# Attention scores through one query-key layer, both images in row tiles, in a software-pipelined token kernel

## The reference

```python
# 1 tokens of an image (192 channels, 14x14 patches)
loc  = dwconv(gelu(conv(x, pl_w, stride=16)))          # layer "L"
g    = gelu(conv(wavelet_packet(x), pg_w1)); g = gelu(dwconv(g))   # layer "G"
glob = conv(g, pg_w2)                                  # layer "W2"
h = (1 - gate) * loc + gate * glob
h = relu(dwconv(h)); h = relu(dwconv(h)); h = dwconv(loc + h)      # "F1", "F2", "F3"
h = concat(cls, layernorm(h) * ln_g + ln_b, txt)       # T = 325 tokens
# 2 attention in a band of 64 tokens, no softmax
n = layernorm(h)
q, k, v = (gelu(n @ w1 + b1) @ w2 + b2 for each of q, k, v)
scores = (q @ k.T) / sqrt(192 * 64) * mask             # mask: 0 <= i - j < 64
h = h + layernorm(scores @ v)
# 3 feed-forward with quantized tokens and ternary weights, hidden width 512
z = rmsnorm(layernorm(h)) ; up, gate = split(quant(z) @ ternary(w_in))
h = h + quant(rmsnorm(silu(gate) * up)) @ ternary(w_out)
```

## Time and profile before

| | |
|---|---|
| median of 3 runs | 1199.82 us (1197.52 to 1203.08) |
| span of the profiled execution | 1195.4 us |
| TensorE busy | 1081.3 us (90% of the span) |
| VectorE busy | 1033.5 us (86%) |
| ScalarE busy | 963.3 us (81%) |
| GpSimd busy | 812.7 us (68%) |

### The profile page before, as it was taken

The page is one execution under the profiler, slowest core; times in us unless marked ns, Lnnn a source line. Parts: engine busy times, 40 slices in busy tenths (PEclk is TensorE's granted clock), DMA queues, the critical chain, the costliest instruction groups (busy, mean ns, idle before and its releaser), DMA issues.

```text
span 1195.4 us, 19559 instructions
## 1 busy us (share of the span) xinstructions
PE 1081.3 (90%) x5674; PEld 736.5 (62%) x5674; DVE 1033.5 (86%) x3013; ACT 963.3 (81%) x2437; POOL 812.7 (68%) x860
## 2 busy tenths in 40 slices
PE   6877999999999999999999999999999897878544
PEld 3655676767676767677676757676766655545311
DVE  1887598999999999999999999999999997856653
ACT  4656687899989898989999988989898978766543
POOL 4446486868687777878686868787786857562521
PEclk9898999999999999999999999999999998979655
DMA  8101010101010100101010101001010000000000
GB/s 327 62 27 41 8 41 7 50 7 57 9 57 9 46 17 16 49 13 50 13 53 7 56 9 54 9 16 50 16 47 15 10 11 15 10 15 9 9 12 14
DMA packets 21513, 40.25 MB, mean 34 GB/s; under 512 B 2656, under 2 KB 18208, under 8 KB 19104
## 3 DMA queue, kind: packets, MB, share of 16 engines
q1 hardware_dynamic: 21408, 39.01, 9.4%
HBM read 31.02 MB, written 7.99 MB: 33 GB/s over the span
## 4 chain that ended last, share of the span: by engine, by line
PE 76%; DVE 9%; ACT 7%; issue 4%; POOL 2%; DMA 1%; SPq 0%; POOLq 0%; DVEq 0%; ACTq 0%
PE bank L398 14%; PE bank L517 7%; PE bank L428 7%; PE bank L439 4%; PE bank L430 4%; PE bank L438 4%; PE bank L376 4%; PE bank L377 3%; PE bank L539 3%; PE bank L458 3%; PE bank L459 3%; DVE bank L1214 2%; PE bank L471 2%; PE bank L472 2%; PE bank L587 2%
## 5 line engine op out<-in xcount | busy, mean ns | idle before, releaser
L1214 DVE SCALAR_TENSOR_TENSOR bank<-padA,c_col,bank 128x406 f32<-128x406 f32 x560 | 357.9, 639 | 7.6
L398 PE MATMUL bank<-x_sb,w_emb 128*128 128x392 f32 x576 | 216.6, 507 | 6.5 <-ACT padA L755 3.7
L810 ACT ACTIVATE prod<-padB,c_col 128x196 f32<-128x196 f32 x432 | 174.3, 449 | 5.1 <-POOL accB L1734 2.5
L1703 POOL TENSOR_TENSOR yg<-y_f,c_gout 128x512 f32<-128x512 f32 (+1 forms) x96 | 122.6, 1278 | 45.9 <-DVE y_f L1404 45.8
L398 PEld LDWEIGHTS bank<-x_sb,w_emb 128*128 128x128 f32 x576 | 102.3, 192 | 60.8 <-ACT padA L755 5.6
L810 ACT ACTIVATE early<-padB,c_col 128x196 f32<-128x196 f32 x288 | 120.7, 449 | 2.3 <-POOL accB L1734 2.2
L517 PE MATMUL bank<-w_in,xq 128*128 128x512 bf16 (+1 forms) x384 | 109.1, 411 | 13.6 <-ACT xq L873 13.6
L1696 POOL TENSOR_TENSOR s<-s,c_mhalf 128x1 f32<-128x1 f32 (+1 forms) x96 | 55.2, 575 | 90.8 <-ACT s L886 90.8
L867 ACT ACTIVATE yq<-bank 128x512 bf16<-128x512 f16 (+1 forms) x96 | 50.2, 523 | 50.8 <-PE bank L529 50.8
L879 ACT ACTIVATE th<-bank,sm 128x512 f32<-128x512 f32 (+1 forms) x96 | 65.3, 681 | 31.6 <-PE bank L517 31.1
L1385 DVE SCALAR_TENSOR_TENSOR ya<-th,bank 128x512 f32<-128x512 f32 (+1 forms) x96 | 65.1, 678 | 26.5 <-ACT th L879 26.3
(11 more groups left out here) (219 smaller groups left out, 3229.3 us busy)
## 6 DMA issues: line engine op xcount, KB each, us to landing
x_sb<-xt SPq DMA_DIRECT2D x16, 1176.0 KB, 5.3
out<-o_sb SPq DMA_DIRECT2D x64, 96.0 KB
w_sq<-squares SPq DMA_DIRECT2D x1, 3840.0 KB, 15.6
h_sb<-txt SPq DMA_DIRECT2D x32, 51.8 KB
out<-o_sb SPq DMA_DIRECT2D x32, 51.8 KB
h_sb<-txt SPq DMA_DIRECT2D x32, 44.2 KB
w_in<-win SPq DMA_DIRECT2D x1, 1024.0 KB, 17.6
c_row<-broads SPq DMA_DIRECT2D x1, 672.0 KB, 19.2
```

What stands on the lines that cost most here:

```text
L398: done = mm(pE[:, 0:2 * N_PATCH], w_emb[:, k, m, :], x_sb[:, k, :], start=k == 0, stop=k == KC - 1)
L810: made = go(grid(prod[ACC[s] ^ 1][:, k, :]), tap_view(padB[min(s, 2)], SIDE, k), ACT.Copy, scale=tapcol(s, 1, k))
L1214: v.scalar_tensor_tensor(grid(acc if k == TAPS - 1 else run), tap_view(pad, ROWS_A, k), tapcol(s, 0, k), grid(run), ALU.mult, ALU.add).the ...
L1703: g.tensor_tensor(yg[0:m, :], y_f[0:m, :], c_gout[0:m, :], ALU.mult).then_inc(f_yg, 1)
```

## The change

- The second query layer q2 goes, with `queries_out`, the tile `q2` and its zeros. Since `q @ k.T = (hq Wq + bq) (hk Wk + bk)^T`, with `hq` and `hk` the hidden layers, a key row becomes `hk (Wk Wq^T)` plus a bias, and is multiplied with `hq` itself; what depends on the key alone is an offset for each key, `hk (Wk bq) + bk.bq`.
- The product of the two weight matrices is made once on the chip: `query_key_weights` on TensorE (transposes of both matrices, the product, the bias columns), after `layer_W2` of pair 0, and `query_key_blocks` on VectorE (copies out of PSUM), after `token_scale_3` and `ternary_weights` and ahead of `mix` of pair 0. The result takes the place of `kw2` in `w_sq`.
- `scores(a)` now makes both images: first nine small products for the key offsets (one or two columns), then, tile by tile, a product over 128 channels for each image and one over 64 partitions (a row tile) for each image, image 0 into one bank and image 1 into the other. The offsets lie in the bank that `values_out(1)` frees.
- VectorE gets `key_offsets` (two small operations, which wait for the scores of image 0), and `scores_out` adds the offset and multiplies by the mask in one operation with a pointer operand.
- The attention now has 23 units, 18 of them ScalarE's (before 26 and 21).
- The lists of all five engines are laid anew. `DEPTH` is 8; the pipeline's stages have the same distances, turn 0 now only loads.

The core of the diff:

```diff
-U_XT, U_Q1, U_K1, U_V1, U_Q2, U_K2, U_V2, U_SC, U_Y = 0, 3, 6, 9, 12, 15, 18, 21, 23
-UNITS = 26
-ACT_UNITS = 21
+U_XT, U_Q1, U_K1, U_V1, U_K2, U_V2, U_SC, U_Y = 0, 3, 6, 9, 12, 15, 18, 20
+UNITS = 23
+ACT_UNITS = 18
...
-            def scores(a, img):
-
-                if img == 0:
-                    took(a, U_K2 + 2)
-                unit_free(a, U_SC + img)
+            def scores(a):
+
+                took(a, U_K2 + 2)
+                unit_free(a, U_SC)
+                for t in range(TILES):
+                    r = pT[U_SC % 2][0:ROWS[t], R_AT + 2 * t:R_AT + 2 * t + 2]
+                    mm(r, hk[:, 2, tok_cols(t)], c_qk[:, 0:2], start=True, stop=False)
+                    for img in range(2):
+                        mm(r[:, img:img + 1], hk[:, img, tok_cols(t)], c_qk[:, 2:3], start=False, stop=img == 1)
+                unit_free(a, U_SC + 1)
                 at = 0
                 for t, n in ((0, SEAM), (1, P + ROWS[2]), (2, ROWS[2])):
-                    dst = pT[(U_SC + img) % 2][0:ROWS[t], at:at + n]
+                    dst = [pT[(U_SC + img) % 2][0:ROWS[t], at:at + n] for img in range(2)]
                     q = slice(t * P, t * P + n)
-                    mm(dst, k2[:, img, tok_cols(t)], q2[:, img, q], start=True, stop=False)
-                    done = mm(dst, k2[:, 2, tok_cols(t)], q2[:, 2 + img, q], start=False, stop=True)
+                    for img in range(2):
+                        mm(dst[img], k2[:, img, tok_cols(t)], hq[:, img, q], start=True, stop=False)
+                    for img in range(2):
+                        done = mm(dst[img], k2[HALF[img], 2, tok_cols(t)], hq[HALF[img], 2, q], start=False, stop=True)
+                        if t == 2:
+                            done.then_inc(at_full, 1)
                     at += n
-                done.then_inc(at_full, 1)
...
+            def query_key_weights():
+
+                pe.wait_ge(s_cst, ALL_CONSTS)
+                cut = (slice(0, P), slice(0, DB))
+                for i, name in enumerate(("qw2", "kw2")):
+                    w = w_sq[:, SQUARES.index(name)]
+                    mm(pT[i][:, 0:P], w[:, AA, :], c_id[:, :], start=True, stop=True)
+                    mm(pT[i][:, P:2 * P], w[:, B0A, :], c_id[:, :], start=True, stop=False)
+                    mm(pT[i][:, P:2 * P], w[:, B1A, :], c_id[:, :], start=False, stop=True)
+                    mm(pT[i][cut[1], 2 * P:3 * P], w[:, AB0, cut[1]], c_id[:, :], start=True, stop=True)
+                    mm(pT[i][cut[1], 3 * P:4 * P], w[:, BB, HALF[0]], c_id[:, :], start=True, stop=False)
+                    done = mm(pT[i][cut[1], 3 * P:4 * P], w[:, BB, HALF[1]], c_id[:, :], start=False, stop=True)
+                done.then_inc(s_qk, 1)
+                pe.wait_ge(s_qkw, 2)
+                for half in range(2):
+                    for o in range(2):
+                        mm(pT[0][:, half * D:(half + 1) * D], t_k2[cut[o], o, half * P:(half + 1) * P],
+                           t_q2[cut[o], o, 0:D], start=o == 0, stop=o == 1)
+                for j, (w, b) in enumerate(((t_k2, "qb2"), (t_k2, "qb2"), (t_q2, "kb2"), (t_q2, "kb2"))):
+                    half = j % 2
+                    for o in range(2):
+                        mm(pT[1][:, j:j + 1], w[cut[o], o, half * P:(half + 1) * P],
+                           colA(b) if o == 0 else colB(b, 0, DB), start=o == 0, stop=o == 1)
+                for o in range(2):
+                    done = mm(pT[1][:, 4:5], c_ones[cut[o], :], c_qk[cut[o], 7 + o:8 + o], start=o == 0, stop=o == 1)
+                done.then_inc(s_qk, 1)
...
+            def keys_out(a, c):
+                took(a, U_K2 + c)
+                go(k2[:, c, :], pT[(U_K2 + c) % 2][:, 0:T], ACT.Identity,
+                   bias=c_qk[:, 4:5] if c < 2 else c_qk[:, 5:6]).then_inc(at_act, 1)
...
-            def queries_out(a, c):
...
             def scores_out(a, img):
 
+                n1, n2 = P + ROWS[2], ROWS[2]
+                if img == 0:
+                    dve.wait_ge(r_saved, a + 1)
                 dve.wait_ge(at_full, a * UNITS + U_SC + img + 1)
...
-                v.tensor_tensor(sc0[:, img, 0:SEAM], src[:, 0:SEAM], c_mask[:, 0:SEAM], ALU.mult)
...
+                v.scalar_tensor_tensor(sc0[:, img, 0:SEAM], src[:, 0:SEAM], r_key[:, 0, img:img + 1], c_mask[:, 0:SEAM],
+                                       ALU.add, ALU.mult)
...
+            def key_offsets(a):
+
+                dve.wait_ge(at_full, a * UNITS + U_SC + 1)
+                if not first(a):
+                    dve.wait_ge(sc_masked, a * 2)
+                n2 = ROWS[2]
+                src = pT[U_SC % 2][:, R_AT:R_AT + 6].rearrange("p (t i) -> p t i", i=2)
+                v.tensor_scalar(r_key[:, 0:2, :], src[:, 0:2, :], c_qk[:, 6:7], None, ALU.add)
+                v.tensor_scalar(r_key[0:n2, 2, :], src[0:n2, 2, :], c_qk[0:n2, 6:7], None, ALU.add).then_inc(r_saved, 1)
```

More of the change, by code:

```diff
@@ L597, in turn @@
+                if on[4]:
+                    mlp_wide(it - 4, 'vw1', U_V1, xT)
+                if on[2]:
+                    layer_L(it - 2)
                 if on[6]:
```

1247 lines of the change are left out of this document (635 added, 612 removed).

## The result

The changed kernel takes 1249.65 us (median; 1245.28 to 1251.22) against 1199.81 us: a ratio of 1.041 (95% interval 1.039 to 1.044). The forecast was 1198.8 us in a range of 1186 to 1211, so the loss of 50 us lies outside of it. The profiled execution has a span of 1249.3 us, 53.9 above the one of before.

A forecast was written before the change was run, and what follows sets the result against it. The prediction took VectorE, with gaps between its dependent steps, as the bound and TensorE right beneath; span 1195.4 + 7 (filling) - 4 (turns) - 4 (draining) = 1194.4, plus 4.4 to the median: 1198.8 us, range 1186 to 1211.

The follow-up runs named there:

- e16: The changed kernel with the weight product moved into waits, offset products ahead of rounded_token_transposes(5) and key_offsets on ScalarE; span 1217.7 us.
- e17: e16 with one entry moved, token_scale_3 two entries earlier on VectorE, ahead of lifted of the last tile; span 1228.6 us.
- e14: The kernel before with unread products on TensorE ahead of the feed-forward's waits in the last pair only; 1191.93 us, ratio 0.995.
- e15: e13 and e14 together: e13 with the unread products in the last pair; 1188.67 us, ratio 0.990 against the kernel before.
- e13: New algorithm in the lists of before, gaps filled by offset and key products, images parted, keys padded, key_offsets on ScalarE, weight product moved; 1195.31 us, ratio 0.996.

## What to carry to other kernels

Before a step is taken off an engine, look at what stood on its two sides in the list: if it filled the time of another engine's round trip, its time isn't saved until something else fills that gap. Two units that share one start and one end are a longer stage for whoever reads them, however little they cost the engine that makes them. A one-time step in the filling belongs where both engines wait, not with a round trip ahead of the first step of the pipeline. And a run that moves a step also moves the signals behind it: look in its trace at what waits for the moved step before reading its time.

## What the runs showed of the hardware

Two of VectorE's operations with two inputs from SBUF took 900 and 1027 ns in the changed kernel, where they end with GpSimd's operation beside them, and 155 and 190 ns before; the first took 896 in e16 and 166 at another place in e17. In the profile that shows as a longer operation, not as idle time. The Trainium skill, "SBUF — State Buffer", section Who interferes with whom, has the rule, as an exclusive lock: a VectorE instruction with two SBUF inputs contends with a GpSimd instruction that reads SBUF. The trace agrees for GpSimd's operations of 392 and 512 columns. It doesn't for one of a single column: beside that (474.84, 0.54 us) VectorE's line 1404, with two inputs too, took 0.17 us at 474.94. The prediction had not weighed the rule.

In the serial feed-forward of the last pair, with TensorE busy 42.8 of 91.0 us, its granted clock was 0.57 in the mean: 1.00 (2.4 GHz) in the first 10 us and 0.50 (1.2 GHz) from 1124 on. Eight unread products a tile raised the mean to 0.80 and took 6 to 7 us off 91 (e14 against before, e15 against e13), without any other change.
